# Joining the w1 products of two tiles in one slot, and f16 products for the half job's w2, in a mixture-of-experts and adapter kernel

## The chip, the cores and the metric

The kernel runs on one core of a Trainium2 chip. The metric is the device time of one execution in microseconds.

## The reference

The input x has 16 batches of 128 tokens with 128 features. The first layer adds to x a mixture of eight gated experts and one shared expert (hidden size 512); the second adds a layer norm over an adapter of rank 32, whose weights are picked by a language id of each batch. Cut to what matters:

```
g = einsum('bsd,edf->ebsf', h, Wg); u = einsum('bsd,edf->ebsf', h, Wu)
expert_outs = einsum('ebsf,efd->ebsd', silu(g) * u, Wd)
x = x + (1 - sg) * einsum('be,ebsd->bsd', gating_probs, expert_outs) + sg * shared
w1 = W1[language_ids]; w2 = W2[language_ids]
h = relu(einsum('bsh,bha->bsa', x, w1) + b1[language_ids])
y = x + einsum('bsa,bah->bsh', h, w2) + b2[language_ids]
x = x + layernorm(y) * gamma[language_ids] + beta[language_ids]
```

In the last line the x that is added and the x inside y are the result of the first layer.

## The kernel before

**Experts.** The tokens are four tiles of four batches (512 columns). The program is a list of 160 steps (STEPS). A step is one tile, one expert and one chunk of 128 hidden units; the steps of tiles 0 and 1 alternate by expert (steps 0 to 71), then come tile 2 (72 to 107) and tile 3 (108 to 159). The last four experts of tile 3 run as two halves of 256 columns, from step 128. In step n TensorE does three f16 products for gate(n), three for up(n) and three for down of an earlier step (three steps back, up to six in the last steps). High and low f16 parts stand in for f32. ACT computes silu(n) and h_hi(n-1), VectorE hidden(n) and h_lo(n-1), and both prepare slices gx_hi and gx_lo of coming experts. gate_ps and up_ps have two banks each, so up(n) waits for hidden(n-2) and gate(n) for silu(n-2).

**Adapter jobs.** JOBS is a table of tile, first batch, number of batches and the step `at` from which the parts of the job are counted. Jobs 0 to 2 are tiles 0 to 2, with `at` 71, 91 and 111; job 3 is the first half of tile 3 (two batches), at 147; the other two batches follow behind the last step (the tail). A whole job goes like this:

- at + 0: ACT makes w2_upper (L586) and VectorE x2T from moe_ps (moe_out, L694).
- at + 1: TensorE does the four w1 products in f32 into adapt_ps (adapter_in, L458), VectorE turn_blocks (L702), then SyncE issues 16 block moves from x2_blocks to x2 (move_blocks, L369), the transposed x2.
- at + 2: ACT four relus (L576), VectorE w2_lower (L706). at + 3: ACT h_upper (L590). at + 4: VectorE h_others, two operations (L712, L713).
- at + 6: TensorE multiplies the stacked f16 h and w2 over 98 rows into x2_ps (adapter_back, L475).
- at + 8: VectorE waits for the moves and makes y (L725), then a statistics and an aggregate per batch in the steps behind. GpSimd adds beta to x2 (x2_beta, L893) once the moves have landed, and the power for rstd (L881).
- at + 14 to at + 18: VectorE makes scaled (L742) and result (L748) per batch.

SyncE's queue is a list in order, for each job: the block moves, a wait for the back products, the weights of the next tile (load_adapter), a wait for the job's results, the store of the tile (L379). It holds:

```
if j < MOVED:
    move_blocks(j)
if t < last_tile:
    sp.wait_ge(back_done, j + 1)
    load_adapter(t + 1)
sp.wait_ge(result_ready, BEFORE[j + 1])
sp.dma_start(out[t, :, first:first + count] ...
```

Job 3 is done otherwise: x2 by two f32 transposes on TensorE (L465) and a copy by ACT (copy_x2, L598), w2 by two f32 products over 33 rows (L482) in two banks, and y per batch (L728). The order in each engine's queue is as written in the loop over n, the parts of a job behind the step's own work; SyncE's queue has no steps and runs by its waits.

In the trace, names lose digits: x is x2, x_blocks is x2_blocks, x_beta is x2_beta, x_ps is x2_ps, w_sb is w1_sb, w_stack is w2_stack, b_sb is b1_sb.

## Time and profile before

| what | value |
|---|---|
| runs | 298.19 us median of 3 (297.6 to 298.32) |
| profiled execution | 297.04 us |
| its span | 295.2 us |
| TensorE, VectorE, ACT, GpSimd busy | 98%, 91%, 78%, 7% of the span |
| chain that ended last | TensorE 94% |
| granted TensorE clock | 0.999 of 2.4 GHz over the span |

The profile comes from one execution. The span is what the engines' records cover, and the execution's own time is 1.84 us longer. Ends of matmuls are modelled, so the start-to-start distance of two products says what one of them costs. An instruction's time includes some overlap with the next one on its engine.

### The profile page before, as it was taken

What the parts mean: (1) busy time and instruction counts of PE and PEld (TensorE: products, weight loads), DVE (VectorE), ACT (ScalarE), POOL (GpSimd) and SP (SyncE); (2) the same over time, 40 slices, a digit from 0 to 9 for tenths busy, and PEclk for the clock granted to TensorE, in tenths of its full rate; (3) what the DMA queues carried; (4) which work ended last, traced back from release to release, by engine and by line L of the source; (5) the groups of instructions that cost most, each with busy time, mean ns of one, the idle gap of its engine ahead of it and who ended that gap; (6) DMA issues with size and microseconds to landing.
All of it is one profiled execution on the core that took longest, in us unless ns stands there. A gap on an engine that the chain in (4) does not pass through costs nothing.

```text
span 295.2 us, 5086 instructions
## 1 busy us (share of the span) xinstructions
PE 290.1 (98%) x1510; PEld 144.3 (49%) x1510; DVE 268.8 (91%) x585; ACT 231.1 (78%) x517; POOL 19.3 (7%) x32
## 2 busy tenths in 40 slices
PE   8999999999999999999999999999999999999995
PEld 2444444444444444444444444444444444588883
DVE  5999999998989898988989999999999999977795
ACT  6998878788878787877897788887878876667771
POOL 3200201100000000000002010001100011000011
PEclk9999999999999999999999999999999999999999
DMA  6973110244000000000011001010001110000001
GB/s 208 385 307 109 52 65 19 62 120 112 2 2 0 0 2 0 0 2 1 1 22 26 18 9 39 12 25 19 17 3 39 27 18 10 2 36 3 0 2 36
DMA packets 17940, 13.39 MB, mean 45 GB/s; under 512 B 11486, under 2 KB 15994, under 8 KB 17914
## 3 DMA queue, kind: packets, MB, share of 16 engines
q1 hardware_dynamic: 17482, 12.86, 14.4%
q8 instruction: 12, 0.20, 0.3%
q10 hardware_dynamic: 432, 0.21, 0.2%
q14 instruction: 14, 0.11, 0.1%
HBM read 11.23 MB, written 1.05 MB: 42 GB/s over the span
## 4 chain that ended last, share of the span: by engine, by line
PE 94%; DVE 2%; DMA 1%; SPq 1%; issue 1%; ACT 0%; POOL 0%; POOLq 0%; DVEq 0%
PE moe_ps L449 10%; PE moe_ps L446 10%; PE moe_ps L447 10%; PE gate_ps L400 10%; PE up_ps L426 10%; PE up_ps L431 10%; PE up_ps L423 10%; PE gate_ps L403 10%; PE gate_ps L408 10%; DMA w_full<-weights 1%; DVE hidden L680 1%; PE adapt_ps L458 0%; DVE gx_lo L649 0%; SPq L319 0%; DVE h_lo L686 0%
## 5 line engine op out<-in xcount | busy, mean ns | idle before, releaser
L563 ACT ACTIVATE silu<-gate_ps 128x512 f32<-128x512 f32 (+1 forms) x160 | 88.2, 551 | 45.3 <-PE gate_ps L408 44.3
L680 DVE SCALAR_TENSOR_TENSOR hidden<-silu,up_ps 128x512 f32<-128x512 f32 (+1 forms) x160 | 100.3, 627 | 19.2 <-PE up_ps L431 11.6
L686 DVE TENSOR_TENSOR h_lo<-hidden,h_hi 128x512 f16<-128x512 f32 (+1 forms) x160 | 102.4, 640 | 0.2
L568 ACT ACTIVATE h_hi<-hidden 128x512 f16<-128x512 f32 (+1 forms) x160 | 92.8, 580 | 9.2 <-DVE hidden L680 8.4
L426 PE MATMUL up_ps<-gx_lo,w_hi 128*128 128x512 f16 (+1 forms) x160 | 57.3, 358 | 0.4 <-DVE gx_lo L649 0.4
L400 PE MATMUL gate_ps<-x_hi,w_hi 128*128 128x512 f16 (+1 forms) x160 | 57.4, 359 | 0.0
L431 PE MATMUL up_ps<-gx_hi,w_lo 128*128 128x512 f16 (+1 forms) x160 | 57.3, 358 | 0.0
L423 PE MATMUL up_ps<-gx_hi,w_hi 128*128 128x512 f16 (+1 forms) x160 | 57.3, 358 | 0.0
L403 PE MATMUL gate_ps<-x_lo,w_hi 128*128 128x512 f16 (+1 forms) x160 | 57.3, 358 | 0.0
L446 PE MATMUL moe_ps<-h_hi,w_hi 128*128 128x512 f16 (+1 forms) x160 | 57.3, 358 | 0.0
L449 PE MATMUL moe_ps<-h_lo,w_hi 128*128 128x512 f16 (+1 forms) x160 | 57.3, 358 | 0.0
L447 PE MATMUL moe_ps<-h_hi,w_lo 128*128 128x512 f16 (+1 forms) x160 | 57.3, 358 | 0.0
L408 PE MATMUL gate_ps<-x_hi,w_lo 128*128 128x512 f16 (+1 forms) x160 | 57.3, 358 | 0.0
L545 ACT ACTIVATE gx_hi<-x_full,coef 128x128 f16<-128x128 f32 x144 | 53.7, 389 | 0.0
L649 DVE SCALAR_TENSOR_TENSOR gx_lo<-x_full,coef,gx_hi 128x128 f16<-128x128 f32 x144 | 50.2, 362 | 0.0
L400 PEld LDWEIGHTS gate_ps<-x_hi,w_hi 128*128 128x128 f16 x160 | 15.6, 98 | 16.5 <-issue 1.4
L423 PEld LDWEIGHTS up_ps<-gx_hi,w_hi 128*128 128x128 f16 x160 | 15.6, 98 | 16.2 <-DVE hidden L680 0.6
L426 PEld LDWEIGHTS up_ps<-gx_lo,w_hi 128*128 128x128 f16 x160 | 15.6, 98 | 15.8 <-DVE gx_lo L649 0.8
L431 PEld LDWEIGHTS up_ps<-gx_hi,w_lo 128*128 128x128 f16 x160 | 15.6, 98 | 15.8 <-DVE w_lo L666 0.5
L449 PEld LDWEIGHTS moe_ps<-h_lo,w_hi 128*128 128x128 f16 x160 | 15.6, 98 | 15.7 <-DVE h_lo L686 0.3
L408 PEld LDWEIGHTS gate_ps<-x_hi,w_lo 128*128 128x128 f16 x160 | 15.6, 98 | 15.4
L403 PEld LDWEIGHTS gate_ps<-x_lo,w_hi 128*128 128x128 f16 x160 | 15.6, 98 | 15.3 <-DVE x_lo L672 0.3
(88 smaller groups left out, 148.6 us busy)
## 6 DMA issues: line engine op xcount, KB each, us to landing
w_full<-weights SPq DMA_DIRECT2D x8, 768.0 KB, 9.2
affine_sb<-affine SPq DMA_DIRECT2D x16, 128.0 KB, 2.9
x_full<-xT SPq DMA_DIRECT2D x3, 256.0 KB, 8.6
x<-x_blocks SPq DMA_DIRECT2D x48, 16.0 KB, 1.8
out_dram<-result SPq DMA_DIRECT2D x3, 256.0 KB, 2.1
w_full<-weights SPq DMA_DIRECT2D x4, 128.0 KB, 3.0
w_full<-w2b SPq DMA_DIRECT2D x24, 16.0 KB
w_full<-weights SPq DMA_DIRECT2D x1, 256.0 KB, 3.8
```

The lines of the kernel that those rows point to most:

```text
L400: nc.tensor.matmul(psum, hi, x_hi[:, x_at], start=True, stop=False)
L403: nc.tensor.matmul(psum, hi, x_lo[:, x_at], start=False, stop=False)
L408: nc.tensor.matmul(psum, lo, x_hi[:, x_at], start=False, stop=True).then_inc(gate_done, 1)
L423: nc.tensor.matmul(psum, hi, gx_hi[:, gx_at], start=True, stop=False)
L426: nc.tensor.matmul(psum, hi, gx_lo[:, gx_at], start=False, stop=False)
L431: nc.tensor.matmul(psum, lo, gx_hi[:, gx_at], start=False, stop=True).then_inc(up_done, 1)
L446: nc.tensor.matmul(psum, hi, hi_slot, start=start, stop=False)
L449: nc.tensor.matmul(psum, hi, lo_slot, start=False, stop=stop).then_inc(down_done, 1)
L563: nc.scalar.activation(silu_slot(n), gate_ps[n % 2][:, 0:STEPS[n][4]], ACT.Silu, scale=1.0 / W_SCALE).then_inc(silu_ready, 1)
L568: nc.scalar.activation(h_slot(h_hi, n), hidden_slot(n), ACT.Copy).then_inc(h_hi_ready, 1)
L680: nc.vector.scalar_tensor_tensor(out=hidden_slot(n), in0=silu_slot(n), scalar=HIDDEN_RESCALE, in1=up_ps[n % 2][:, 0:STEPS[n][4]], op0=ALU. ...
L686: nc.vector.tensor_tensor(h_slot(h_lo, n), hidden_slot(n), h_slot(h_hi, n), ALU.subtract).then_inc(h_lo_ready, 1)
```

## The change

Three things:

1. JOBS[0] is counted from step 75 instead of 71. The new moe_at keeps x2T of tile 0 in step 71, and puts that of tile 1 in step 75 (91 before). The new in_step puts the w1 products of jobs 0 and 1 both in step 76 (72 and 92 before). For this x2T, w1_sb and b1_sb have a second place, used by tile 1, and tile 1's products go into columns 128 to 255 of adapt_ps.
2. SyncE loads w1 and b1 of tile 1 at the start, right behind tile 0's weights, and only w2 of tile 1 behind the first job's back products.
3. Job 3 uses the f16 path for w2: w2_upper in step 139, w2_lower in 141, h_upper in 151, h_others in 152, two f16 products over 98 rows in step 154 (two f32 products in 153 before), y as one operation in 155. Four loads of w2 per batch replace one for its two batches. All widths follow the job's number of batches.

```diff
-JOBS = [(0, 0, BATCHES, down_step(0, 0) + 1), (1, 0, BATCHES, down_step(0, 0) + 21),
+JOBS = [(0, 0, BATCHES, down_step(1, 0) + 1), (1, 0, BATCHES, down_step(0, 0) + 21),
...
+def moe_at(j):
+    return down_step(JOBS[j][0], 0) + 1
+def in_step(j):
+    return JOBS[0 if j == 1 else j][3] + in_at(j)
...
 def back_at(j):
-    return 6
+    return 6 if j < MOVED else 7
+def w2_at(j):
+    return 0 if j < MOVED else -8
...
-            def load_adapter(t):
+            def load_adapter(t, first, second):
...
-            load_adapter(0)
+            load_adapter(0, True, True)
+            load_adapter(1, True, False)
...
-                    load_adapter(t + 1)
+                    load_adapter(t + 1, t > 0, True)
...
             def adapter_in(j):
...
-                pe.wait_ge(adapter_loaded, adapter_count(t))
-                if j > 0:
+                pe.wait_ge(adapter_loaded, adapter_count(0 if t == 1 else t))
+                if j > 1:
                     pe.wait_ge(y_ready, BEFORE[j])
                 for q in range(first, first + count):
-                    last = nc.tensor.matmul(fourth(adapt_ps, q)[:, 0:S], cols(w1_sb, q, A), cols(x2T, q, S),
+                    last = nc.tensor.matmul(cols(fourth(adapt_ps, q), place(t), S, A), w1_of(t, q), cols(x2T_of(t), q, S),
...
             def adapter_back(j):
...
-                pe.wait_ge(adapt_h_ready, count)
-                pe.wait_ge(x2_ready, 1)
+                if j >= MOVED:
+                    pe.wait_ge(x2_ready, 1)
                 for q in range(first, first + count):
-                    last = nc.tensor.matmul(cols(back_ps[q % 2], q // 2, D), stacked(adapt_h, q, S, A + 1),
-                                            stacked(w2b2_sb, q, D, A + 1), start=True, stop=True)
+                    last = nc.tensor.matmul(cols(x2_ps, q, D), cols(h_stack, q, S, STACK), cols(w2_stack, q, D, STACK),
+                                            start=True, stop=True)
...
-                    if n == at + in_at(j):
+                    if n == in_step(j):
                         adapter_in(j)
...
-                    if n == at and j < MOVED:
+                    if n == at + w2_at(j):
                         w2_upper(j)
...
-                    if n == at + in_at(j) + 2 and j < MOVED:
+                    if n == at + in_at(j) + 2:
                         h_upper(j)
...
-                if j > 0:
+                if j > 1:
                     dve.wait_ge(adapt_done, j)
                     dve.wait_ge(blocks_ready, j)
-                nc.vector.scalar_tensor_tensor(out=x2T[:, :], in0=moe_ps[t % 2][:, :], scalar=OUT_RESCALE,
+                nc.vector.scalar_tensor_tensor(out=x2T_of(t), in0=moe_ps[t % 2][:, :], scalar=OUT_RESCALE,
...
-                if since == 4 and j < MOVED:
+                if since == in_at(j) + 3:
                     h_others(j)
...
-                for j, (_, _, _, at) in enumerate(JOBS):
-                    if n == at:
+                for j in range(len(JOBS)):
+                    if n == moe_at(j):
                         moe_out(j)
```

What this moves in the queues stands in the next lists, which give the order on one engine. VectorE before, from tile 0's last result (L748, step 89) over moe_out of tile 1 (L694, step 91) to turn_blocks of tile 1 (L702, step 92):

```order
L748 SCALAR_TENSOR_TENSOR result<-scaled,rstd,x_beta 128x128
L680 SCALAR_TENSOR_TENSOR hidden<-silu,up_ps 128x512
L686 TENSOR_TENSOR h_lo<-hidden,h_hi 128x512
L649 SCALAR_TENSOR_TENSOR gx_lo<-x_full,coef,gx_hi 128x128
L680 SCALAR_TENSOR_TENSOR hidden<-silu,up_ps 128x512
L694 SCALAR_TENSOR_TENSOR x2T<-moe_ps,x_full 128x512
L686 TENSOR_TENSOR h_lo<-hidden,h_hi 128x512
L649 SCALAR_TENSOR_TENSOR gx_lo<-x_full,coef,gx_hi 128x128 x2
L680 SCALAR_TENSOR_TENSOR hidden<-silu,up_ps 128x512
L686 TENSOR_TENSOR h_lo<-hidden,h_hi 128x512
L649 SCALAR_TENSOR_TENSOR gx_lo<-x_full,coef,gx_hi 128x128
L702 STREAM_TRANSPOSE x_blocks<-x2T 128x512
```

VectorE now, steps 92 and 93 (L704 is hidden, L710 h_lo, L673 gx_lo, L774 result, L768 scaled, L726 turn_blocks, L731 w2_lower):

```order
L704 SCALAR_TENSOR_TENSOR hidden<-silu,up_ps 128x512
L710 TENSOR_TENSOR h_lo<-hidden,h_hi 128x512
L673 SCALAR_TENSOR_TENSOR gx_lo<-x_full,coef,gx_hi 128x128
L774 SCALAR_TENSOR_TENSOR result<-scaled,rstd,x_beta 128x128
L768 SCALAR_TENSOR_TENSOR scaled<-y,moments,affine_sb 128x128
L726 STREAM_TRANSPOSE x_blocks<-x2T 128x512
L704 SCALAR_TENSOR_TENSOR hidden<-silu,up_ps 128x512
L710 TENSOR_TENSOR h_lo<-hidden,h_hi 128x512
L673 SCALAR_TENSOR_TENSOR gx_lo<-x_full,coef,gx_hi 128x128
L774 SCALAR_TENSOR_TENSOR result<-scaled,rstd,x_beta 128x128
L731 SCALAR_TENSOR_TENSOR w_stack<-w_full,w_stack 33x512
```

Tile 0's last result stood three steps ahead of tile 1's turn_blocks, and now stands one step behind it.

ACT before, steps 150 to 152 (L563 silu, L568 h_hi, L579 the relus, L598 copy_x2):

```order
L563 ACTIVATE silu<-gate_ps 128x256
L568 ACTIVATE h_hi<-hidden 128x256
L579 ACTIVATE adapt_h<-adapt_ps,b_sb 32x128 x2
L563 ACTIVATE silu<-gate_ps 128x256
L568 ACTIVATE h_hi<-hidden 128x256
L598 ACTIVATE x<-x_ps 128x256
L563 ACTIVATE silu<-gate_ps 128x256
```

ACT now, the same steps (L587 silu, L592 h_hi, L599 the relus, L613 h_upper, L622 copy_x2):

```order
L587 ACTIVATE silu<-gate_ps 128x256
L592 ACTIVATE h_hi<-hidden 128x256
L599 ACTIVATE h_full<-adapt_ps,b_sb 32x128 x2
L587 ACTIVATE silu<-gate_ps 128x256
L592 ACTIVATE h_hi<-hidden 128x256
L613 ACTIVATE h_stack<-h_full 32x256
L622 ACTIVATE x<-x_ps 128x256
L587 ACTIVATE silu<-gate_ps 128x256
```

One more operation stands between silu(151) and silu(152).

## Rows read from the trace of the kernel before

**Rows 1.** The page, busy us (share of the span) xinstructions of each engine.

```profile
PE 290.1 (98%) x1510; PEld 144.3 (49%) x1510; DVE 268.8 (91%) x585; ACT 231.1 (78%) x517; POOL 19.3 (7%) x32
```

**Rows 2.** Timeline (start us, us, engine line op) of PE: up(93), up(100), up(102).

```profile
186.53 0.38 PE L431 MATMUL up_ps<-gx_hi,w_lo 128*128 128x512 f16 x1
...
200.35 0.38 PE L431 MATMUL up_ps<-gx_hi,w_lo 128*128 128x512 f16 x1
...
203.80 0.38 PE L423 MATMUL up_ps<-gx_hi,w_hi 128*128 128x512 f16 x1
```

**Rows 3.** Timeline of DVE: steps 89 to 93, then hidden(99) to hidden(100).

```profile
181.62 0.34 DVE L748 SCALAR_TENSOR_TENSOR result<-scaled,rstd,x_beta 128x128 f32<-128x128 f32 x1
181.88 0.67 DVE L680 SCALAR_TENSOR_TENSOR hidden<-silu,up_ps 128x512 f32<-128x512 f32 x1
...
183.35 0.67 DVE L680 SCALAR_TENSOR_TENSOR hidden<-silu,up_ps 128x512 f32<-128x512 f32 x1
...
187.13 0.69 DVE L702 STREAM_TRANSPOSE x_blocks<-x2T 128x512 f32<-128x512 f32 x1
187.76 0.64 DVE L680 SCALAR_TENSOR_TENSOR hidden<-silu,up_ps 128x512 f32<-128x512 f32 x1
...
199.38 0.68 DVE L680 SCALAR_TENSOR_TENSOR hidden<-silu,up_ps 128x512 f32<-128x512 f32 x1
199.98 1.34 DVE L686 TENSOR_TENSOR h_lo<-hidden,h_hi 128x512 f16<-128x512 f32 x1
...
201.50 0.68 DVE L725 SCALAR_TENSOR_TENSOR y<-x_ps,x 128x512 f32<-128x512 f32 x1
...
202.49 0.67 DVE L680 SCALAR_TENSOR_TENSOR hidden<-silu,up_ps 128x512 f32<-128x512 f32 x1
```

**Rows 4.** Timeline of PE around tile 0's w1 products.

```profile
145.18 0.38 PE L449 MATMUL moe_ps<-h_lo,w_hi 128*128 128x512 f16 x1
...
145.84 0.39 PE L400 MATMUL gate_ps<-x_hi,w_hi 128*128 128x512 f16 x1
```

**Rows 5.** Timeline of PE around tile 0's f16 back products.

```profile
155.35 0.38 PE L449 MATMUL moe_ps<-h_lo,w_hi 128*128 128x512 f16 x1
...
155.79 0.38 PE L400 MATMUL gate_ps<-x_hi,w_hi 128*128 128x512 f16 x1
```

**Rows 6.** Timeline of PE around the half job's f32 back products.

```profile
280.62 0.27 PE L449 MATMUL moe_ps<-h_lo,w_hi 128*128 128x256 f16 x1
...
281.25 0.28 PE L400 MATMUL gate_ps<-x_hi,w_hi 128*128 128x256 f16 x1
```

**Rows 7.** Timeline of PE and PEld, up(153), with the idle time before it.

```profile
280.06 0.10 PEld L423 LDWEIGHTS up_ps<-gx_hi,w_hi 128*128 128x128 f16 x1 [0.23 <-DVE hidden L680]
```

**Rows 8.** Timeline of ACT: copy_x2 and silu(152).

```profile
279.90 0.37 ACT L598 ACTIVATE x<-x_ps 128x256 f32<-128x256 f32 x1
280.16 0.38 ACT L563 ACTIVATE silu<-gate_ps 128x256 f32<-128x256 f32 x1
```

**Rows 9.** Timeline of DVE: hidden(152).

```profile
280.57 0.42 DVE L680 SCALAR_TENSOR_TENSOR hidden<-silu,up_ps 128x256 f32<-128x256 f32 x1
```

**Rows 10.** Timeline of SP: block moves of tiles 0, 1, 2; store of tile 0.

```profile
147.37 11.62 SPq L369 DMA_DIRECT2D x<-x_blocks  x16
...
181.99 0.38 SPq L379 DMA_DIRECT2D out_dram<-result  x1
187.86 10.32 SPq L369 DMA_DIRECT2D x<-x_blocks  x16
...
227.09 10.84 SPq L369 DMA_DIRECT2D x<-x_blocks  x16
```

**Rows 11.** Timeline of POOL: x2_beta of the three tiles.

```profile
160.35 1.85 POOL L893 TENSOR_TENSOR x_beta<-x,affine_sb 128x512 f32<-128x512 f32 x1 [107.27 <-DMA x<-x_blocks]
...
199.50 1.27 POOL L893 TENSOR_TENSOR x_beta<-x,affine_sb 128x512 f32<-128x512 f32 x1 [27.78 <-DMA x<-x_blocks]
...
239.23 1.27 POOL L893 TENSOR_TENSOR x_beta<-x,affine_sb 128x512 f32<-128x512 f32 x1 [28.30 <-DMA x<-x_blocks]
```

More of the change, by code:

```diff
@@ L200, in build @@
         x2_ps = bank("x2_ps")
-        back_ps = [adapt_ps, x2_ps]
         last_tile = TILES - 1
@@ L276, in adapter_count, with place, w1_of, b1_of @@
         def adapter_count(t):
-            return 16 * BATCHES * (6 * (t + 1) if t < last_tile else 6 * t + 3)
+            return 16 * (8 * BATCHES, 12 * BATCHES, 18 * BATCHES, 18 * BATCHES + 6 * (BATCHES - TAIL[2]) + 3 * TAIL[2])[t]
+        def place(t):
+            return 1 if t == 1 else 0
+        def w1_of(t, q):
+            return cols(w1_sb, place(t) * BATCHES + q, A)
+        def b1_of(t, q):
+            return fourth(b1_sb, q)[:, place(t):place(t) + 1]
+        def x2T_of(t):
+            return cols(x2T, place(t), N)
         def fourth(tensor, q):
@@ L342, in load_adapter @@
                     one = bass.ds(lang, 1)
-                    sp.dma_start(cols(w1_sb, q, A), w1[one].rearrange("l h a -> (l h) a")).then_inc(adapter_loaded, 16)
+                    if first:
+                        sp.dma_start(w1_of(t, q), w1[one].rearrange("l h a -> (l h) a")).then_inc(adapter_loaded, 16)
+                        sp.dma_start(b1_of(t, q), b1[one].rearrange("l a o -> (l a) o")).then_inc(adapter_loaded, 16)
                     w2b2_q = w2b2[one].rearrange("l a h -> (l a) h")
-                    if t == last_tile:
+                    if second and t == last_tile and q >= TAIL[1]:
                         sp.dma_start(stacked(w2b2_sb, q, D, A + 1), w2b2_q).then_inc(adapter_loaded, 16)
-                    else:
+                    elif second:
                         w2_q = cols(w2_full, q, D, STACK)
@@ L519, in _ @@
                 if i == 0:
-                    pe.wait_ge(adapt_h_ready, JOBS[-1][2] + 1)
+                    pe.wait_ge(adapt_h_ready, 1)
                 else:
@@ L585, in w2_upper @@
                     act.wait_ge(back_done, j)
-                nc.scalar.activation(w2_stack[:, :], w2_full[:, :], ACT.Copy, scale=W_SCALE).then_inc(w2_upper_ready, 1)
+                width = JOBS[j][2] * D
+                nc.scalar.activation(w2_stack[:, 0:width], w2_full[:, 0:width], ACT.Copy,
+                                     scale=W_SCALE).then_inc(w2_upper_ready, 1)
             def h_upper(j):
                 act.wait_ge(h_full_ready, BEFORE[j + 1])
-                nc.scalar.activation(h_stack[0:A, :], h_full[:, :], ACT.Copy, scale=H_SCALE).then_inc(h_upper_ready, 1)
+                width = JOBS[j][2] * S
+                nc.scalar.activation(h_stack[0:A, 0:width], h_full[:, 0:width], ACT.Copy,
+                                     scale=H_SCALE).then_inc(h_upper_ready, 1)
             def copy_x2(j):
@@ L701, in turn_blocks @@
                     dve.wait_ge(x2_moved, 16 * BLOCKS * BLOCKS * j)
-                nc.vector.transpose(x2_blocks[:, :], x2T[:, :]).then_inc(blocks_ready, 1)
+                nc.vector.transpose(x2_blocks[:, :], x2T_of(JOBS[j][0])).then_inc(blocks_ready, 1)
             def w2_lower(j):
                 dve.wait_ge(w2_upper_ready, j + 1)
-                nc.vector.scalar_tensor_tensor(out=w2_stack[2 * A:STACK - 1, :], in0=w2_full[2 * A:STACK - 1, :], scalar=W_SCALE,
-                                               in1=w2_stack[2 * A:STACK - 1, :], op0=ALU.mult,
+                width = JOBS[j][2] * D
+                nc.vector.scalar_tensor_tensor(out=w2_stack[2 * A:STACK - 1, 0:width], in0=w2_full[2 * A:STACK - 1, 0:width],
+                                               scalar=W_SCALE, in1=w2_stack[2 * A:STACK - 1, 0:width], op0=ALU.mult,
                                                op1=ALU.subtract).then_inc(w2_lower_ready, 1)
@@ L755, in job_part @@
                     turn_blocks(j)
-                if since == 2 and j < MOVED:
+                if since == w2_at(j) + 2:
                     w2_lower(j)
-                if since == 4 and j < MOVED:
+                if since == in_at(j) + 3:
                     h_others(j)
```

44 lines of the change are left out of this document (17 added, 27 removed).

## The prediction

> **What bounds the kernel now.** I read the page first. TensorE is busy for 290.1 of the span's 295.2 us [rows 1], so the time is TensorE's list of products plus its pauses, and an edit counts only if it shortens that list or makes TensorE wait. But VectorE is busy 91% of the span and runs only a little ahead of need. So the second thing to read is how late VectorE is in each step, and the third is who can make it late: SyncE's queue and GpSimd.
>
> A full step is nine f16 products. The last product of up(93) starts at 186.53 and that of up(100) at 200.35 [rows 2], seven steps and one f16 back group apart. The group is priced in the next paragraph at 0.22, which leaves 13.60, or **1.94 us a step**, 0.216 a product of 512 columns and 0.108 one of 256. VectorE's own plain step (hidden, h_lo, one gx_lo) runs from 181.88 to 183.35, 1.47 us; one slice of 128 columns (result, here 181.62 to 181.88) is 0.26 [rows 3]. With six or seven such extras a step is over 1.94, and VectorE falls behind.
>
> **Part 1, the w1 products.** Before, the last down product starts at 145.18 and the next gate product at 145.84 [rows 4]: 0.66, less the product's own 0.216, so the slot of four f32 products costs TensorE 0.44. The f16 back group takes 155.79 - 155.35 - 0.216 = 0.22 for four products [rows 5]. Now tiles 0 and 1 share a slot (step 76), and the one of step 92 is gone. Two slots cost 0.89; the joint one costs 0.44 plus its second four products. These cost something between 0 (all beside the first four) and 0.44 (all over again). I take half, 0.22, because a slot holds products and the way in and out, and the way is now paid once. **Gain 0.22**, bounds 0 and 0.44. Nothing waits for tile 1's x2T there: it is written in step 75, one step ahead of the slot, as tile 0's was before, and the w1 loads are issued tens of us earlier.
>
> **Part 2, the half job's w2 products.** Two f32 products of 33 rows lie between 280.62 and 281.25 [rows 6]: 0.63 - 0.108 = 0.52. Two f16 products cost half of the 0.22 above, 0.11. TensorE's list gets **0.41 shorter**. The work that this needs is on engines that are late just there. In these steps TensorE already waits 0.23 for hidden, before up(153) at 280.06, because ACT had the relus in front of silu [rows 7]. The change puts h_upper (32x256) in front of copy_x2 and silu(152). copy_x2 to silu(152) was 0.26 [rows 8]; another such entry moves silu(152) from 280.16 to about 280.45 and hidden(152), which started 0.41 behind it at 280.57 and took 0.42 [rows 9], to 280.86 to 281.28. Behind it VectorE has h_lo (0.33, somewhat over half of the 0.60 from 199.38 to 199.98 that an operation on 512 columns takes up [rows 3]) and the new h_others, two operations together about 0.6 (an estimate: two of that same width at the 0.26 to 0.33 above), so hidden(153) ends near 282.6. Without waiting TensorE would start up(155) at 281.25 - 0.52 + 0.98 + 0.11 + 0.33 = 282.15; it has to wait until 282.6, and before it started at 281.25 + 0.98 + 0.33 = 282.56. So I put this part at **0**. Bounds: -0.41 if the new work fits in, +0.3 if one more entry of each engine is late. The w2_upper and w2_lower of this job stand in steps 139 and 141, where both engines have idle time in each step, and cost nothing. The norm of the job starts one step later and its y is one operation in place of two; the tail behind the last product is the same.
>
> **Part 3, tile 0's job four steps later.** This is the part that costs. JOBS[0] moves from step 71 to 75, so its results leave in steps 90 to 93 instead of 86 to 89. SyncE's list is in order: the store of tile 0, then the 16 block moves of tile 1, for which VectorE's y in step 99 waits. Before, the store went out at 181.99 and the moves at 187.86, as soon as turn_blocks (187.13 to 187.76) had ended [rows 3, 10]: SyncE was waiting for VectorE. Now the moves stand behind tile 0's last result, in step 93, one step after turn_blocks.
>
> How late is VectorE there? The lag is the start of hidden(n) less the end of up(n) (its last product's start and 0.38). After y it is 202.49 - 200.73 = 1.76; hidden(100), 0.67 long, could have started 0.64 later without stopping up(102), which starts at 203.80, so the latest lag is 2.40 [rows 2, 3]. For the new tile 0 job I take 1.9 in step 84, near the first of the two. From there, in steps 84 to 92, VectorE has nine plain steps (13.2), three second gx_lo slices (0.78), three statistics and four aggregates (0.9, an estimate: about 0.3 for one of each, by what lies between y's 0.68 and hidden(100)), four scaled and three result slices (1.82) and turn_blocks (0.63): 17.3 against 17.5 of TensorE. So the lag at step 93 is 1.7, where it was 187.76 - 186.91 = 0.85 before. up(93) now ends at 186.91 - 0.22 = 186.69, hidden(93) starts at 188.4, and the result ends 1.47 + 0.34 later, at **190.2**. The store follows at once, the first move about 0.5 later, at 190.7, against 187.86 before.
>
> From the first move to the start of GpSimd's x2_beta, which waits for the last one, went 12.98, 11.64 and 12.14 us for the three tiles [rows 10, 11]. So the blocks are there at 203.7, 202.3 or 202.8; I take 12.14, the middle one. y started at 201.50 and hidden(100) 0.99 later [rows 3], so hidden(100) now starts at 203.8 and ends at 204.5. up(102) started at 203.80 [rows 2] and would now start at 203.58. **TensorE waits 0.9**, between 0.4 and 1.8. What else VectorE is late by in steps 94 to 98 (w2_lower and h_others fall on the larger lag) is part of this wait and not added: the moves set a fixed hour. Tile 2's loads and moves have some us to spare, and job 0's own moves and y keep their distance of seven steps.
>
> One thing is given back here. Before, the h_lo that started at 199.98, inside GpSimd's x2_beta (199.50, 1.27 long), took 1.34 instead of 0.68 [rows 3, 11]. Now x2_beta and y start together, and the next h_lo comes 1.6 us later, after x2_beta's end. Whether y itself is held is another matter, since no row shows an operation of its form that starts inside x2_beta. The Trainium skill (SBUF — State Buffer, Who interferes with whom) says that a VectorE instruction with two SBUF inputs is blocked for the whole of a GpSimd instruction that reads SBUF, and one with at most one SBUF input is not. The stretched h_lo agrees; y reads one input from PSUM, so by the page it is free and the sum stays. Were it held, the rival below is the price.
>
> **Sum.** -0.22 + 0 + 0.9 = **+0.7 us**. The profiled execution took 297.04 us, its span 295.2, the median of the runs is 298.19 (297.6 to 298.32). The sum gives 297.7 for a profiled execution and **298.9** against the median.
>
> **Rivals.**
> 1. *The wait does not form.* If VectorE is less late than my ledger says (lag 0.85, as before) the moves start 0.8 earlier, and with 11.64 us they are there at 201.5, when y is reached anyway. For it: VectorE sheds 0.47 in each plain step, and my 1.9 in step 84 is a choice. Against it: seven slices of 0.26 now lie in the steps where turn_blocks does. Then the gains stand: -0.22 to -0.63, 297.6 to 298.0.
> 2. *Clearly slower: y is held by GpSimd.* It decides if y (one PSUM, one SBUF input) cannot start inside x2_beta. Both are released by the same transfers, so y would lose x2_beta's 1.27: +0.7 + 1.27 = +2.0, 300.2. Against it: hidden, of the same form, started at 199.38 and ran its usual 0.68 while x2_beta began beside it [rows 3, 11]; but it had started first.
> 3. *Faster beyond the bound:* all of 0.44 and 0.41 arrives, and no wait: 297.3. Against it: TensorE's wait at 280.06, and that VectorE had only 0.64 to spare after y.
>
> **How the numbers follow.** A measurement of this kernel tells 0.3%, 0.9 us, from no change. The forecast case has 0.6; with its bounds it gives 298.2 to 299.9, a little over half of it under 299.1: 0.33 same, 0.27 slower. Rival 1 has 0.22, same. Rival 2 has 0.12, slower. Rival 3 has 0.06, faster. Together: faster 0.06, same 0.55, slower 0.39. The range that leaves out rival 3 and what lies above rival 2 is 297.6 to 300.2. The likeliest is 298.9.
>
> **What would show it.** In the profile after: one joint group of w1 products near 153 us, and the gap around it near 0.88 (0.66 plus 0.22); no gap in step 92. Tile 0's store near 190 us, tile 1's first block move within 1 us behind it, and x2_beta near 202.8. A pause of TensorE before up(102), released by VectorE's hidden, of 0.4 us or more. Near 280 us two f16 products in 0.11, but a longer wait for hidden before up(154) and up(155). I am wrong if x2_beta of tile 1 starts before 202 us, if no pause stands there, or if the pauses near 280 us stay at what they were.

## The result and the profile after

The changed kernel takes **298.62 us** (median of 19 runs, 298.12 to 299.5), the kernel before 297.57 us (19 runs, 296.87 to 298.34). The ratio is 1.0037, with the interval 1.0029 to 1.0045: **slower by 1.1 us**, 0.9 to 1.3. The forecast was 0.7 us and 298.9. So the loss is a little above the 0.3% that a measurement can tell, in the case that had 0.39 of the chance and not in the one that had 0.55. The profiled execution took 298.45 us, its span 296.7 us.

The page after, busy time of each engine and the chain that ended last:

```profile
PE 290.6 (98%) x1508; PEld 144.0 (49%) x1508; DVE 269.3 (91%) x587; ACT 231.8 (78%) x519; POOL 18.7 (6%) x32
...
PE 81%; DVE 11%; issue 4%; ACT 3%; POOL 0%; POOLq 0%; DVEq 0%; ACTq 0%
```

Against [rows 1] nothing stands out: TensorE has two instructions fewer (the half job's two f32 back products show as four instructions, the two f16 ones as two) and VectorE and ACT two more each. A loss of 1 us can't be read from sums over 295 us. So I follow one instruction of every step, the last product of up(n), through both traces. Its start after, less its start before, is the **shift** at step n; where it jumps, time went or came. Here it is at the steps where it changes, before at L431, after at L461:

| step n | before | after | shift | change of it | what stands there |
|---|---|---|---|---|---|
| 40 | 82.37 | 82.81 | 0.44 | | start-up, the same products in both |
| 73 | 146.93 | 146.91 | -0.02 | -0.46 | tile 0's own slot of w1 products is gone |
| 77 | 154.70 | 155.36 | 0.66 | +0.68 | the joint slot |
| 78 | 156.87 | 157.30 | 0.43 | -0.23 | tile 0's back products are no longer here |
| 82 | 164.69 | 165.30 | 0.61 | +0.18 | but here, +0.23; and -0.05, a pause that only the trace of before has |
| 93 | 186.53 | 186.67 | 0.14 | -0.46 | tile 1's own slot is gone |
| 96 | 192.35 | 192.72 | 0.37 | +0.23 | a pause before up(96) |
| 98 | 196.46 | 197.34 | 0.88 | +0.51 | a pause before tile 1's back products |
| 153 | 280.30 | 281.17 | 0.87 | -0.01 | |
| 154 | 281.81 | 282.44 | 0.63 | -0.24 | no f32 back products any more |
| 155 | 282.79 | 284.20 | 1.41 | +0.78 | a pause before the f16 ones |
| 159 | 286.72 | 288.13 | 1.41 | 0 | |

The 0.44 at step 40 belongs to the execution, not to the change: up to there the products are the same. The change also loads w1 and b1 of tile 1 early, but the shift is 0.44 from step 4 on (12.44 us before, 12.88 after), and SyncE issues its first adapter load only at 39.4 and 39.7 us. So the change costs 1.41 - 0.44 = **0.97 us** in this trace: up to step 93 it gains 0.30, steps 94 to 98 cost 0.74, and the half job costs 0.53. Of the 0.30 the slots give 0.25. The other 0.05 is a pause before up(82) in the profiled execution of before, whose weight load waited 0.37 there for hidden; with tile 0's job in its old step (experiment 1, the half job alone) it is gone too.

The joint slot, timeline of PE of the kernel after (start us, us, engine, line, operation):

```profile
153.38 0.38 PE L479 MATMUL moe_ps<-h_lo,w_hi 128*128 128x512 f16 x1
153.69 0.64 PE L488 MATMUL adapt_ps<-x2T,w_sb 128*32 128x128 f32 x16
154.27 0.39 PE L430 MATMUL gate_ps<-x_hi,w_hi 128*128 128x512 f16 x1
```

From the last down product to the next gate product it is 0.89, forecast 0.88; in [rows 4] a single slot had 0.66.

Now VectorE, where the loss is. Timeline of DVE of the kernel after, steps 93 to 97 (in brackets the idle time before an instruction and what ended it; there is none until y):

```profile
188.30 0.70 DVE L726 STREAM_TRANSPOSE x_blocks<-x2T 128x512 f32<-128x512 f32 x1
188.93 0.65 DVE L704 SCALAR_TENSOR_TENSOR hidden<-silu,up_ps 128x512 f32<-128x512 f32 x1
...
190.36 0.34 DVE L774 SCALAR_TENSOR_TENSOR result<-scaled,rstd,x_beta 128x128 f32<-128x128 f32 x1
190.73 0.69 DVE L731 SCALAR_TENSOR_TENSOR w_stack<-w_full,w_stack 33x512 f16<-33x512 f32 x1
191.45 0.69 DVE L704 SCALAR_TENSOR_TENSOR hidden<-silu,up_ps 128x512 f32<-128x512 f32 x1
...
194.76 0.42 DVE L738 TENSOR_SCALAR h_stack<-h_full 32x512 f16<-32x512 f32 x1
195.21 0.68 DVE L740 SCALAR_TENSOR_TENSOR h_stack<-h_full,h_stack 32x512 f16<-32x512 f32 x1
195.92 0.69 DVE L704 SCALAR_TENSOR_TENSOR hidden<-silu,up_ps 128x512 f32<-128x512 f32 x1
...
202.88 0.69 DVE L753 SCALAR_TENSOR_TENSOR y<-x_ps,x 128x512 f32<-128x512 f32 x1 [0.76 <-DMA x<-x_blocks]
...
203.88 0.67 DVE L704 SCALAR_TENSOR_TENSOR hidden<-silu,up_ps 128x512 f32<-128x512 f32 x1
204.47 0.68 DVE L710 TENSOR_TENSOR h_lo<-hidden,h_hi 128x512 f16<-128x512 f32 x1
```

And TensorE over the same stretch, timeline of PE of the kernel after:

```profile
188.61 0.38 PE L461 MATMUL up_ps<-gx_hi,w_lo 128*128 128x512 f16 x1
190.12 0.38 PE L453 MATMUL up_ps<-gx_hi,w_hi 128*128 128x512 f16 x1
...
192.29 0.38 PE L453 MATMUL up_ps<-gx_hi,w_hi 128*128 128x512 f16 x1
192.72 0.38 PE L461 MATMUL up_ps<-gx_hi,w_lo 128*128 128x512 f16 x1
...
196.04 0.38 PE L506 MATMUL x_ps<-w_stack,h_stack 98*128 98x128 f16 x4 [0.35 <-DVE h_stack L740]
...
197.34 0.38 PE L461 MATMUL up_ps<-gx_hi,w_lo 128*128 128x512 f16 x1
```

hidden(94) starts at 191.45, which is 191.45 - 188.61 - 0.38 = 2.46 behind the end of up(94); before it was 1.16. up(96) can't start until it has ended, and starts 2.17 behind up(95) in place of 1.94: the 0.23. Then h_others of tile 1 (L738, L740) end at 195.89, and tile 1's back products start at 196.04; that is the 0.51. In step 93 alone VectorE needs 191.45 - 188.93 = 2.52 us for one step of 1.94, since tile 0's result slice and tile 1's w2_lower both stand in it; before the change tile 0's results had left by step 89.

What the queues did, timelines of SP and POOL of the kernel after:

```profile
190.73 0.38 SPq L409 DMA_DIRECT2D out_dram<-result  x1
191.22 10.28 SPq L399 DMA_DIRECT2D x<-x_blocks  x16
```

```profile
202.82 1.27 POOL L919 TENSOR_TENSOR x_beta<-x,affine_sb 128x512 f32<-128x512 f32 x1 [22.95 <-DMA x<-x_blocks]
```

Against [rows 10, 11] the first move is 3.4 us later. VectorE's y waited 0.76 for it. But TensorE has no jump between steps 98 and 153: nobody paid for that wait.

The half job, timelines of ACT, DVE and PE of the kernel after:

```profile
280.78 0.40 ACT L613 ACTIVATE h_stack<-h_full 32x256 f16<-32x256 f32 x1
281.09 0.36 ACT L622 ACTIVATE x<-x_ps 128x256 f32<-128x256 f32 x1
281.35 0.36 ACT L587 ACTIVATE silu<-gate_ps 128x256 f32<-128x256 f32 x1
```

```profile
281.74 0.42 DVE L704 SCALAR_TENSOR_TENSOR hidden<-silu,up_ps 128x256 f32<-128x256 f32 x1 [0.40 <-ACT silu L587]
...
282.56 0.29 DVE L738 TENSOR_SCALAR h_stack<-h_full 32x256 f16<-32x256 f32 x1
282.87 0.41 DVE L740 SCALAR_TENSOR_TENSOR h_stack<-h_full,h_stack 32x256 f16<-32x256 f32 x1
283.32 0.42 DVE L704 SCALAR_TENSOR_TENSOR hidden<-silu,up_ps 128x256 f32<-128x256 f32 x1
```

```profile
282.77 0.27 PE L479 MATMUL moe_ps<-h_lo,w_hi 128*128 128x256 f16 x1
283.54 0.27 PE L506 MATMUL x_ps<-w_stack,h_stack 98*128 98x128 f16 x2 [0.50 <-DVE h_stack L740]
283.65 0.27 PE L430 MATMUL gate_ps<-x_hi,w_hi 128*128 128x256 f16 x1
```

```profile
281.76 0.10 PEld L430 LDWEIGHTS gate_ps<-x_hi,w_hi 128*128 128x128 f16 x1 [0.27 <-ACT silu L587]
...
282.21 0.10 PEld L453 LDWEIGHTS up_ps<-gx_hi,w_hi 128*128 128x128 f16 x1 [0.23 <-DVE hidden L704]
```

(The last fence is PEld, TensorE's weight loads.) Step 154 is shorter by 0.24 only. The f32 products (0.52) are gone from it, but by the starts of its products TensorE now loses 0.15 before gate(154), which waits for silu(152) behind ACT's new h_upper, and 0.12 before up(154), which waits for hidden(152) behind that silu. (The brackets in the last fence are the idle time of the weight loads, which run ahead of the products; what TensorE loses is the distance between two products, less the plain 0.11.) One step later h_others end at 283.28 and the two back products start at 283.54. From the last down product to the next gate product it is 0.88, where the f32 ones had 0.63 [rows 6], though the two take 0.11 as forecast.

### The profile page after: what moved, and what is told of

It reads as the page before. It is cut to its first block, busy times and chain, and to the rows that moved or that the text cites. A ratio compares the mean times of both kernels' runs of the same rounds, so it can differ in the third digit from the quotient of the medians.

```text
span 296.7 us, 5113 instructions
## 1 busy us (share of the span) xinstructions
PE 290.6 (98%) x1508; PEld 144.0 (49%) x1508; DVE 269.3 (91%) x587; ACT 231.8 (78%) x519; POOL 18.7 (6%) x32
## 3 DMA queue, kind: packets, MB, share of 16 engines
HBM read 11.30 MB, written 1.05 MB: 42 GB/s over the span
## 4 chain that ended last, share of the span: by engine, by line
PE 81%; DVE 11%; issue 4%; ACT 3%; POOL 0%; POOLq 0%; DVEq 0%; ACTq 0%
PE gate_ps L430 9%; PE moe_ps L479 9%; PE moe_ps L477 9%; PE moe_ps L476 9%; PE gate_ps L438 9%; PE gate_ps L433 9%; PE up_ps L456 9%; PE up_ps L461 9%; PE up_ps L453 8%; DVE h_lo L710 3%; DVE gx_lo L673 3%; DVE hidden L704 2%; PE moe_ps L512 1%; ACT h_hi L592 1%; ACT silu L587 1%
## 5 line engine op out<-in xcount | busy, mean ns | idle before, releaser
L587 ACT ACTIVATE silu<-gate_ps 128x512 f32<-128x512 f32 (+1 forms) x160 | 88.1, 550 | 42.2 <-PE gate_ps L438 41.2
L704 DVE SCALAR_TENSOR_TENSOR hidden<-silu,up_ps 128x512 f32<-128x512 f32 (+1 forms) x160 | 100.3, 627 | 19.2 <-PE up_ps L461 12.4
L592 ACT ACTIVATE h_hi<-hidden 128x512 f16<-128x512 f32 (+1 forms) x160 | 92.9, 580 | 12.7 <-DVE hidden L704 12.2
L710 DVE TENSOR_TENSOR h_lo<-hidden,h_hi 128x512 f16<-128x512 f32 (+1 forms) x160 | 100.9, 631 | 0.2
L461 PE MATMUL up_ps<-gx_hi,w_lo 128*128 128x512 f16 (+1 forms) x160 | 57.3, 358 | 0.0
L673 DVE SCALAR_TENSOR_TENSOR gx_lo<-x_full,coef,gx_hi 128x128 f16<-128x128 f32 x144 | 51.4, 371 | 0.0
L461 PEld LDWEIGHTS up_ps<-gx_hi,w_lo 128*128 128x128 f16 x160 | 15.7, 98 | 15.7 <-DVE w_lo L690 0.6
L476 PEld LDWEIGHTS moe_ps<-h_hi,w_hi 128*128 128x128 f16 x160 | 15.7, 98 | 15.4 <-DVE w_lo L690 0.4
```

Of the source, the lines that this page charges most:

```text
L461: nc.tensor.matmul(psum, lo, gx_hi[:, gx_at], start=False, stop=True).then_inc(up_done, 1)
L476: nc.tensor.matmul(psum, hi, hi_slot, start=start, stop=False)
L587: nc.scalar.activation(silu_slot(n), gate_ps[n % 2][:, 0:STEPS[n][4]], ACT.Silu, scale=1.0 / W_SCALE).then_inc(silu_ready, 1)
L592: nc.scalar.activation(h_slot(h_hi, n), hidden_slot(n), ACT.Copy).then_inc(h_hi_ready, 1)
L704: nc.vector.scalar_tensor_tensor(out=hidden_slot(n), in0=silu_slot(n), scalar=HIDDEN_RESCALE, in1=up_ps[n % 2][:, 0:STEPS[n][4]], op0=ALU. ...
L710: nc.vector.tensor_tensor(h_slot(h_lo, n), hidden_slot(n), h_slot(h_hi, n), ALU.subtract).then_inc(h_lo_ready, 1)
```

## The experiments

Three theories stood at the start. **M**, the prediction's: the store of tile 0 holds up tile 1's block moves, and that fixed hour sets the loss in steps 94 to 102. **V**: VectorE's backlog itself, since the jobs of tiles 0 and 1 now start 16 steps apart instead of 20, and the moves are innocent. For the half job **A**: only the back products' wait for h_others; **B**: too many entries on ACT and VectorE there, whoever is waited for. For each kernel I give the timed ratio to the kernel before, measured beside it, and the trace's figure: the shift at step 159 less the shift at step 40. The second is the finer one, since it leaves the start-up out.

### 1. Each part alone

The first kernel keeps the joint slot and has the half job as before (f32 products, 33 rows); the second has the f16 half job, with tile 0's job back at its old step:

```diff
# e1_slot_only, against the changed kernel: the half job's lines of before
-    return 6 if j < MOVED else 7
+    return 6
...
-                    last = nc.tensor.matmul(cols(x2_ps, q, D), cols(h_stack, q, S, STACK), cols(w2_stack, q, D, STACK),
-                                            start=True, stop=True)
+                    last = nc.tensor.matmul(cols(back_ps[q % 2], q // 2, D), stacked(adapt_h, q, S, A + 1),
+                                            stacked(w2b2_sb, q, D, A + 1), start=True, stop=True)
# e2_half_only, against the changed kernel
-JOBS = [(0, 0, BATCHES, down_step(1, 0) + 1), ...
+JOBS = [(0, 0, BATCHES, down_step(0, 0) + 1), ...
 def in_step(j):
-    return JOBS[0 if j == 1 else j][3] + in_at(j)
+    return JOBS[j][3] + in_at(j)
```

> The kernel before with the joint slot alone (job 0 counted from step 75, w1 products of tiles 0 and 1 in step 76, second places), the half job as it was. Theory A (VectorE's backlog in steps 93 to 97 stops TensorE, the trace of the changed kernel shows 0.23 before up(96) and 0.51 before tile 1's back products, against 0.30 gained by the slot): +0.44 us against before, and the same two pauses. Theory B (the slot part pays, and all of the loss comes from the half job): -0.3 us, and no pause near step 96.

> The changed kernel with job 0 counted from step 71 and tile 0's and tile 1's w1 products in steps of their own, so of the change only the half job's f16 w2 (and the second places and the order of the loads) are left. Theory A (the half job loses by itself: its back products stand in TensorE's queue before gate(155) and wait for h_others): +0.5 us against before. Theory B (the half job only loses because the whole pipeline arrives late from the part before): at most 0, down to -0.4.

The slot alone: 298.3 us against 297.67, ratio 1.0015 (1.0002 to 1.0028); in the trace +0.59: -0.30 up to step 93, +0.24 at step 96, +0.51 at 98, and a further +0.14 at 102 and 103, where this time y's wait for the moves (0.92 here) does reach TensorE. The half job alone: 298.16 us, 1.0005 (0.999 to 1.002); the timing shows no difference, the trace +0.49: -0.24 at step 154 and +0.78 at 155, as in the changed kernel, and the -0.05 at step 82. So the two parts are independent, and each is a loss of about half a microsecond by its trace.

### 2. The block moves ahead of the store

```diff
# e3_moves_first
-                if j < MOVED:
+                if j < MOVED and j != 1:
...
+                if j == 0:
+                    move_blocks(1)
```

> The changed kernel with one thing in another order on SyncE: tile 1's 16 block moves ahead of tile 0's store, so they wait for turn_blocks alone. Theory A (TensorE had lost its time in steps 94 to 97 before y waited for the moves, so the wait of y stops nobody): +1.0 us against before as the changed kernel, y no longer waits 0.76, TensorE's pauses stay. Theory M, as my prediction had it (the moves' hour sets the loss): the 0.7 us come back, +0.3 us against before.

298.76 us, ratio 1.0027 (1.0015 to 1.004); in the trace +0.99. Timelines of SP, POOL and DVE of this kernel:

```profile
189.49 10.28 SPq L399 DMA_DIRECT2D x<-x_blocks  x16
```

```profile
201.05 1.27 POOL L921 TENSOR_TENSOR x_beta<-x,affine_sb 128x512 f32<-128x512 f32 x1 [20.73 <-DMA x<-x_blocks]
```

```profile
201.63 1.23 DVE L712 TENSOR_TENSOR h_lo<-hidden,h_hi 128x512 f16<-128x512 f32 x1
...
203.05 0.68 DVE L755 SCALAR_TENSOR_TENSOR y<-x_ps,x 128x512 f32<-128x512 f32 x1
```

The execution started 0.44 later than that of the changed kernel, so the moves went out 2.2 us earlier by the step. y waits for nothing, and the pauses of TensorE are what they were: +0.23 at step 96, +0.51 at 98, none at 102. **M falls** as the cause of this loss. A second thing is in these rows: x2_beta now starts earlier and the h_lo that runs beside it takes 1.23 in place of 0.68, so what y doesn't wait VectorE pays there.

### 3. The back products a step later

```diff
# e4_back3_later: the half job's back products one step later
-    return 6 if j < MOVED else 7
+    return 6 if j < MOVED else 8
# e5_back1_later: those of tile 1
-    return 6 if j < MOVED else 7
+    return (6, 7, 6, 7)[j]
```

(The statistics of tile 1 keep their step in the second; a third kernel is the second with the moves ahead of the store.)

> The changed kernel with the half job's two back products (and all that follows them in the job) one step later, in step 155. Theory A (they hold up TensorE only by their place in the queue, h_others ends at 283.28 and they stand before gate(155)): 0.4 to 0.6 us below the changed kernel, about +0.5 against before. Theory B (VectorE and ACT are overloaded there by the new operations, so the wait only moves to hidden before up(155)): no more than 0.2 below the changed kernel, +0.8 to +1.0 against before.

> The changed kernel with tile 1's (only tile 1's) back products one step later, in step 98, y still in 99. In the changed kernel they stood before gate(98) and waited 0.5 us for h_others. One theory: the backlog alone costs, so the 0.5 us come back. Mine now: two limits of nearly the same hour stand one behind the other, h_others in step 97 and the block moves in step 99, so TensorE gains 0.5 at the back products and loses 0.3 to 0.5 of it before up(102), where hidden(100) comes late because y waited for the moves.

> e5_back1_later with tile 1's block moves ahead of tile 0's store as well. If two limits stand one behind the other, only both together give the time back: TensorE's pause before the back products and the one before up(102) are both gone, 0.3 to 0.5 us less in its timeline than e5_back1_later, while the moves first alone gave nothing. If the moves never mattered, the same as e5_back1_later within 0.1.

The half job: 298.79 us, ratio 1.0027 (1.0011 to 1.0042), trace +0.93, the half job's part +0.49 in place of +0.53. The wait has only changed its name, timeline of PE:

```profile
284.45 0.28 PE L453 MATMUL up_ps<-gx_hi,w_hi 128*128 128x256 f16 x1 [0.42 <-DVE hidden L704]
...
285.12 0.28 PE L506 MATMUL x_ps<-w_stack,h_stack 98*128 98x128 f16 x2
```

That is B. Tile 1's: 298.31 us in one run against 297.61, trace +1.00; with the moves first 298.15 us, trace +0.96. Nothing gained, and my expectation failed: I thought that 0.5 would be won at step 98 and lost before up(102). It is lost at once, timelines of PEld and DVE of the kernel with tile 1's products later:

```profile
196.50 0.10 PEld L453 LDWEIGHTS up_ps<-gx_hi,w_hi 128*128 128x128 f16 x1 [0.83 <-DVE hidden L704]
```

```profile
195.76 0.69 DVE L704 SCALAR_TENSOR_TENSOR hidden<-silu,up_ps 128x512 f32<-128x512 f32 x1
```

hidden(96) ends at 196.4 whether the back products wait or not, and up(98) needs it. Steps 94 to 99 cost +0.23, +0.29 and +0.22 here, the same 0.74 (the back products' own 0.22 has only moved from step 98 to 99). A late engine collects the same toll from whatever stands next.

### 4. Which work makes the half job late

```diff
# e8_no_h_upper: ACT's operation left out in the half job
-                    if n == at + in_at(j) + 2:
+                    if n == at + in_at(j) + 2 and j < MOVED:
# e9_no_h_others: VectorE's two left out in the half job
-                if since == in_at(j) + 3:
+                if since == in_at(j) + 3 and j < MOVED:
```

> The changed kernel without ACT's h_upper in the half job (the upper part of h for tile 3's first two batches stays that of the tile before, so that part of the output is left out); h_others waits for the relus. If ACT's one more operation is what costs there, the half job's 0.53 us loss turns into a gain of 0.2 to 0.4. If VectorE's h_others is the cost, only ACT's 0.3 comes back, so about 0.2 us of loss is left.

> The changed kernel without VectorE's two h_others operations in the half job (the lower parts of its h are left out); the back products wait for h_upper. If VectorE's h_others is the cost, steps 154 and 155 lose nothing any more and the half job gains 0.2 to 0.4 us against before, since the wait before gate(154) and up(154) for ACT's silu stays. If ACT is the cost, at least 0.3 us of the loss stays.

(Each engine that loses its releaser waits for the operation before it. In the second, adapter_back has one wait more for every job.)

One run each, 298.14 and 298.61 us; the trace has the half job's part at +0.24 without h_upper (-0.52 at step 154, +0.76 at 155) and at -0.12 without h_others (-0.24, +0.12, and the 0.12 is no pause but the two products' own 0.11). So of the loss of 0.53, ACT's one operation is 0.29 and VectorE's two are 0.65; together they outdo the gain of the shorter list, 0.41. The first was as expected. The second gained less than the 0.2 to 0.4 that I gave it, though I had ACT's wait in it: -0.41 + 0.29 is -0.12, and I had not added it up. In the second kernel the back products of tile 1 also start 0.11 later than in the changed kernel (step 98 has +0.62 in place of +0.51); the wait that was added there is the only difference of the two in that stretch.

### 5. Moving VectorE's work within the stretch

From here on the half job is as before the change, the slot as in the first experiment.

```diff
# e7_slot_out_early, against e1_slot_only: scaled and result of tile 0 two steps earlier
-                out_at = stats_at(j) + count + (2 if j < MOVED else 0)
+                out_at = stats_at(j) + count + (0, 2, 2, 0)[j]
```

> The joint slot alone (e1_slot_only) with tile 0's scaled and result slices two steps earlier, in steps 87 to 91 instead of 89 to 93, so that none stands in the steps of turn_blocks and w2_lower of tile 1. If the collision of these slices with tile 1's job is the cause of the loss, VectorE's lag at hidden(94) falls from 2.5 to about 1.9, TensorE has no pause in steps 96 to 102, and its timeline is 0.3 us shorter than before's from step 72 to the end: 0.9 us less than e1_slot_only's, 0.3 us below before in the time, which is at the edge of what a timing can tell. If the loss comes from elsewhere (the joint slot itself, the later job, the loads), it stays within 0.2 us of e1_slot_only.

298.31 us, ratio 1.0023 (1.001 to 1.0036), trace +0.44. **My expectation failed**: the pauses at steps 96 and 98 are +0.23 and +0.51 again. Timeline of DVE:

```profile
188.55 0.71 DVE L725 STREAM_TRANSPOSE x_blocks<-x2T 128x512 f32<-128x512 f32 x1
189.18 0.65 DVE L703 SCALAR_TENSOR_TENSOR hidden<-silu,up_ps 128x512 f32<-128x512 f32 x1
...
191.45 0.69 DVE L703 SCALAR_TENSOR_TENSOR hidden<-silu,up_ps 128x512 f32<-128x512 f32 x1
```

hidden(94) starts at the same 191.45, 2.47 behind up(94). The eight slices were done earlier, and lifted the lag earlier: in step 90 it is 1.91 in place of 0.86. VectorE is never idle from step 88 to 97, so the sum of its work up to step 94 is what counts, not its order. Only the 0.14 at steps 102 and 103 went, since the store and the moves (first at 189.29) come earlier too; M's wait is real, but small.

### 6. The jobs at their old distance

```diff
# e10_jobs_later, against e1_slot_only: jobs start at steps 75, 95, 115
-(1, 0, BATCHES, down_step(0, 0) + 21), (2, 0, BATCHES, down_step(2, 0) + 1)
+(1, 0, BATCHES, down_step(0, 0) + 25), (2, 0, BATCHES, down_step(2, 0) + 5)
# e11_job1_later: 75, 95, 111
+(1, 0, BATCHES, down_step(0, 0) + 25), (2, 0, BATCHES, down_step(2, 0) + 1)
```

> e1_slot_only with jobs 1 and 2 counted from steps 95 and 115 instead of 91 and 111, so that the three jobs are 20 steps apart again, as before; x2T of tiles 1 and 2 and the joint slot stay in steps 75, 111 and 76. If the loss is that VectorE has to do the same two jobs in 16 steps instead of 20 and never catches up in between, no pause of TensorE is left in steps 84 to 104, and its timeline from step 40 to the end is 0.3 us shorter than before's (the slot's gain), 0.9 less than e1_slot_only's; the time 0.1 to 0.5 below before. If the joint slot or the later job 0 costs by itself, the loss stays.

> e1_slot_only with job 1 alone counted from 95; job 2 stays at 111, so the 16 steps now lie between jobs 1 and 2. By the same theory the pauses in steps 94 to 102 go, and the backlog comes back in steps 113 to 121; it is smaller there, because the gx_lo slices end at step 120: a loss of 0 to 0.5 us there, in the timeline -0.3 to +0.2 against before. If nearness of the jobs is not the cause, all pauses stay where they were.

With 20 steps between all three jobs no pause is left: trace **-0.30**, the same as the changed kernel's up to step 93, and the lag at step 94 is 1.05, at 96 0.35 (2.46 and 2.82 in the changed kernel). Tile 1's moves are free here too: the store goes out at 191.34, the first move at 196.61 and behind turn_blocks alone, so this kernel removes M's wait together with V's, and that V is the cause rests on experiments 2 and 5. The timing has 297.78 us against 297.64, ratio 1.0008 (0.9994 to 1.0022). Moving only tile 1's job moves the crowding to tiles 1 and 2: 299.44 us, ratio 1.0068 (1.0051 to 1.0085), trace +0.84. The pauses stand 20 steps on, timelines of PE and DVE of that kernel:

```profile
234.73 0.38 PE L454 MATMUL up_ps<-gx_hi,w_lo 128*128 128x512 f16 x1
237.41 0.38 PE L454 MATMUL up_ps<-gx_hi,w_lo 128*128 128x512 f16 x1
...
243.24 0.38 PE L454 MATMUL up_ps<-gx_hi,w_lo 128*128 128x512 f16 x1
245.70 0.38 PE L454 MATMUL up_ps<-gx_hi,w_lo 128*128 128x512 f16 x1
```

```profile
243.52 0.69 DVE L748 SCALAR_TENSOR_TENSOR y<-x_ps,x 128x512 f32<-128x512 f32 x1 [1.32 <-DMA x<-x_blocks]
```

up(117) to up(118) takes 2.68, up(121) to up(122) 2.46, where [rows 2] and the paragraph on them gave 1.94 (before, the first of these had its 0.22 of back products within it: 2.17). The second is M's wait at last: y is 1.32 late and TensorE pays 0.52. So three kernels give a scale, each behind 0.6 to 0.75 that TensorE had already lost: y waits 0.76 and TensorE pays nothing (0.77 to 0.79 and nothing in four others), 0.92 and it pays 0.14, 1.32 and it pays 0.52. VectorE could lose about 0.8 there for free, in that state. I had expected up to 0.5 in this kernel, and the trace shows 1.14 between steps 116 and 122.

### 7. The best I could put together

e10_jobs_later, with copy_x2 of the half job two steps earlier and its two relus in two steps, so that ACT has no pile near 280 us:

```diff
# e12_best, against e10_jobs_later
-                    if n == at + in_at(j) + 1:
+                    if n == at + in_at(j) + 1 and j < MOVED:
                         adapter_relu(j)
+                    for i in range(JOBS[j][2]):
+                        if n == at + in_at(j) + 1 + i and j >= MOVED:
+                            adapter_relu(j, JOBS[j][1] + i)
...
-                    if n == at + in_at(j) + 2 and j >= MOVED:
+                    if n == at + in_at(j) and j >= MOVED:
```

> e10_jobs_later with ACT's work for the half job in another order: copy_x2 in step 149, where ACT waited 0.77 us for the gate products, and the two relus in steps 150 and 151 instead of both in 150. The relus kept silu(151) back, and that made TensorE wait about 0.35 us before gate(153) and up(153). If so, that pause goes and the timeline is 0.6 to 0.65 us shorter than before's, the time 0.3 to 0.9 us below before. If VectorE or the slot is what holds there, it equals e10_jobs_later.

Trace -0.44: the 0.30 of e10_jobs_later and about 0.15 at step 153, of the 0.6 and more expected. The pause went, but it was short. Timeline of PE of the kernel before:

```profile
279.84 0.27 PE L408 MATMUL gate_ps<-x_hi,w_lo 128*128 128x256 f16 x1
280.06 0.28 PE L423 MATMUL up_ps<-gx_hi,w_hi 128*128 128x256 f16 x1
```

From product to product it is 0.22 where 0.11 is plain, so 0.11 was lost, and two products beside it lost 0.01 to 0.02 each. The 0.23 in [rows 7], which I had added up, is idle time of the weight loads. Timing: 297.66 us against 297.64, ratio 1.0001 (0.9987 to 1.0015). It is no faster than the kernel before, and none of the twelve is. A part of the difference between trace and timing is at the other end of the program: in every kernel with the slot and the f32 half job (this one, and experiments 1, 5 and 6) the span ends 2.32 to 2.37 us after the issue of the last store, in the kernel before, in the changed kernel and in all with the f16 half job 1.94 to 2.04. With that 0.4 the trace gives -0.04 here and +0.07 for e10_jobs_later, both within the intervals; e11_job1_later comes to 1.2 against 1.5 at least, which stays open, as does the first kernel, 1.0 against 0.8 at most.

## Why the prediction was right in its number, and where it was wrong

**Part 1, right.** Gain 0.22 forecast, about 0.25 measured (0.92 for two slots, less 0.68 for the joint one). The trace has 0.30, with 0.05 from the pause before up(82) that is no part of the slots. The joint slot's second four products cost about half as much as the first four, as I had taken.

**Part 3, the right size for the wrong reason.** The profiled execution started 0.44 later than that of before, so 0.44 goes off each of its times. Then the forecast hours came out within 0.4: result end 190.2, measured 190.3; first move 190.7, measured 190.8; x2_beta 202.8, measured 202.4 (it came 11.6 behind the first move, not 12.14); hidden(100) 203.8, measured 203.4. The loss was put at 0.9 and is 0.74. But the step "What else VectorE is late by in steps 94 to 98 ... is part of this wait and not added: the moves set a fixed hour" failed. The loss was taken by VectorE's backlog in steps 96 and 98, before y was reached, and having lost 0.74 there TensorE was late enough that y's wait of 0.76 stopped nobody. Bringing the moves forward gave nothing back (experiment 2, and 5 with +0.23 and +0.51 and no wait of y); giving the jobs their distance back gave it all (experiment 6). The predicted wait stood behind the real one as a second limit of nearly the same size. Had TensorE lost nothing by step 98, up(100) would have ended at 200.35 + 0.38 + 0.14 = 200.87, the lag of hidden(100) at 203.88 would have been 3.01, and by the prediction's 2.40 TensorE would have waited 0.6 for it (an estimate; no run has the late moves without the backlog). So that 0.9 was near 0.74 is luck. I had the lag of step 93 right (1.7 forecast, 1.88 measured) and stopped one step short: a result slice and w2_lower stand between hidden(93) and hidden(94), so the lag at step 94 is 2.46, over the 2.40 that the prediction itself had called the latest that stops nobody. The sign to look for, a pause before up(102), was named wrongly: there is none in this trace, and the prediction had said "I am wrong [...] if no pause stands there".

**Part 2, mis-sized.** The half job was put at 0, bounds -0.41 and +0.3; it cost **+0.53**, outside the bounds. The shorter list came as forecast, and so did ACT's part: hidden(152) was to start at 280.86, and 280.86 + 0.87 (the shift at step 153) is 281.73, measured 281.74. The step that failed is "it has to wait until 282.6", for hidden(153). The back products wait earlier in TensorE's list, for h_others, and behind them stand their own 0.11 and a gate product of 0.33 before up(155). With the prediction's own numbers h_others ended at 280.86 + 0.33 + 0.33 + 0.6 = 282.12; add the 0.26 from their end to the back products' start (283.28 to 283.54) and the 0.44, and up(155) starts at 282.82 in place of 282.56: +0.26. The other 0.3 are two durations: h_lo, which waits for ACT's h_hi, took 0.49 to the next start and not 0.33, and h_others took 0.72 (282.56 to 283.28) and not 0.6. One reading was wrong besides and changed nothing in the sum: "TensorE already waits 0.23 for hidden" is idle time of the weight loads, and TensorE lost 0.11 there (experiment 7).

**The sum.** -0.30 + 0.74 + 0.53 = +0.97 measured in the trace, -0.22 + 0.9 + 0 = +0.7 forecast: part 3 a little high, part 2 half a microsecond low. That the time itself, 298.9, is so near the measured 298.62 is partly luck: it was counted from a median of three runs, 298.19, and 19 runs have 297.57. The forecast loss was 0.7, the measured one 1.1.

**Rivals.** 1, the wait does not form: no, VectorE was as late as the ledger said. 2, y held by GpSimd: no; y started at 202.88 beside x2_beta (202.82 to 204.09) and took 0.69. The Trainium skill (SBUF — State Buffer, Who interferes with whom) says that a VectorE instruction with at most one SBUF input, outside the 2-port perf modes, does not contend with GpSimd; the trace agrees for y and hidden. 3, faster: no, though experiment 6 shows that its slot half was to be had in TensorE's list, though the timing doesn't show it.

## What to carry to other kernels

When an engine is busy without a gap through a stretch, its backlog is the sum of its work up to that point: moving work within the stretch, or letting somebody else wait for it, changes the name of the wait and not its length. What helps is the distance between two bursts. Moving one of several evenly spaced jobs to save a slot on the bound engine crowds its neighbour, so move them all or none. And before pricing a cheaper form of an operation on the bound engine, list what prepares it, on which engines, and in which step: 0.41 less in TensorE's list was paid with 0.94 of its waiting for two engines that were late just there.

## What the runs showed of the hardware

**h_lo and gx_lo are stretched by GpSimd, y and hidden aren't.** The h_lo that started inside x2_beta took 1.34 [rows 3] and 1.23 (experiment 2) against 0.68. gx_lo does the same: in the changed kernel, inside tile 2's x2_beta (240.82 to 242.17), it took 1.36 in place of 0.34. Timeline of DVE of the kernel after:

```profile
240.97 1.36 DVE L673 SCALAR_TENSOR_TENSOR gx_lo<-x_full,coef,gx_hi 128x128 f16<-128x128 f32 x1
```

y and hidden beside x2_beta kept 0.67 to 0.69, also when y started inside it. h_lo and gx_lo read two tiles of SBUF, the others one of PSUM and one of SBUF. It goes the other way too: x2_beta took 1.85 in place of 1.27 when it started at 160.35 [rows 11], just ahead of an h_lo (160.39) that kept its 0.68; GpSimd's spans are rough.

**Start-up differs from one execution to the next by more than most of these changes.** At step 40 the twelve experiments and the changed kernel were 0.08 to 1.62 us behind the profiled run of the kernel before, with the same products up to there, and all of that by step 4. That run was itself 0.5 us under its median. A comparison of two spans can't resolve 0.5 us; the shift of one instruction against itself can.

**The end of the program.** Where the span ended 0.4 later after the last store's issue, the DMA view has a transfer that the others lack. Behind 296 us, of the kernel of experiment 1 (queue, kind: packets, MB, share):

```profile
q14 instruction: 1, 0.01, 0.7%
```

All five kernels with the longer end (that one and those of experiments 5, 6 and 7) have this one transfer there; the other nine, those before and after the change among them, have none of that queue behind 292 us. The programs differ in length: 5097 or 5098 instructions in the five, 5086 before, 5113 to 5116 in the others. That the last piece of code is fetched late there, and that it costs the 0.4, is a guess that fits; no run was made for it.
